# Attention inside two quantized feed-forward layers: Q and K in one step of row tiles, V and P·V moved between the quarters of a head pair

## The reference

```python
x = x + 0.5 * ffn(layernorm(x), w_gate, w_up, w_down)      # first layer
x = x + attn(layernorm(x), ...)                            # attention
x = x + 0.5 * ffn(layernorm(x), w_gate, w_up, w_down)      # last layer

# ffn: every operand is rounded to an 8-value grid in blocks of 16
h = silu(q(x) @ q(w_gate).T) * (q(x) @ q(w_up).T)          # 352 wide
return q(h) @ q(w_down).T

# attn: 16 heads of 64
q, k, v = x @ w_q, x @ w_k, x @ w_v                        # 128 -> 1024 each
attn = softmax(q @ k.T / 8)
y = (attn @ v) @ w_proj + b_proj + x
return layernorm(y) * ln_gamma + ln_beta
```

## Time and profile before

| | |
|---|---|
| median of 3 runs | 2265.52 us (2261.74 to 2266.74) |
| the profiled execution | 2263.16 us, of which the span is 2261.4 us |
| TensorE busy | 2142.7 us, 95% of the span |
| VectorE busy | 1605.5 us, 71% |
| GpSimd busy | 1407.7 us, 62% |
| ScalarE busy | 1151.4 us, 51% |
| mean granted TensorE clock | 0.978 |

### The profile page before, as it was taken

The page is one execution under the profiler, slowest core; times in us unless marked ns, Lnnn a source line. Parts: engine busy times, 40 slices in busy tenths (PEclk is TensorE's granted clock), DMA queues, the critical chain, the costliest instruction groups (busy, mean ns, idle before and its releaser), DMA issues.

```text
span 2261.4 us, 38387 instructions
## 1 busy us (share of the span) xinstructions
PE 2142.7 (95%) x14537; PEld 1094.4 (48%) x14537; DVE 1605.5 (71%) x2609; ACT 1151.4 (51%) x1749; POOL 1407.7 (62%) x1289
## 2 busy tenths in 40 slices
PE   3899999999999999999999999999999999999974
PEld 2344444545445454545545454554544545454432
DVE  5565767767687786868777686877778687776634
ACT  2455554645555454555545455455555545454532
POOL 3365666757576675757756576675757667665642
PEclk8799999999999999999999999999999999999986
DMA  1000000000000000000000000000000000000000
GB/s 60 1 7 2 6 2 2 12 2 7 7 7 7 2 11 2 7 7 7 7 2 11 2 7 7 2 12 2 10 3 6 7 2 12 2 2 7 2 7 10
DMA packets 167493, 15.83 MB, mean 7 GB/s; under 512 B 148304, under 2 KB 166928, under 8 KB 167312
## 3 DMA queue, kind: packets, MB, share of 16 engines
q1 hardware_dynamic: 167312, 13.39, 5.1%
HBM read 7.03 MB, written 4.19 MB: 5 GB/s over the span
## 4 chain that ended last, share of the span: by engine, by line
PE 85%; DVE 6%; SPq 2%; issue 2%; POOL 2%; DMA 1%; ACT 1%; POOLq 0%; DVEq 0%
PE pS L934 23%; PE pO L961 20%; PE pM L918 9%; PE pX L946 5%; PE pM L1077 5%; PE pX L985 5%; PE pM L973 3%; PE LpF L333 2%; PE FpF L333 2%; SPq L568 2%; PE FpF L296 2%; PE LpF L296 2%; PE LpF L309 2%; PE FpF L309 2%; PE LpF L324 1%
## 5 line engine op out<-in xcount | busy, mean ns | idle before, releaser
L676 POOL TENSOR_TENSOR ES<-ES,E 128x512 f32<-128x512 f32 x512 | 654.9, 1300 | 217.1 <-ACT E L747 209.9
L747 ACT ACTIVATE E<-pS 128x1024 f32<-128x1024 f32 x512 | 523.2, 1022 | 459.9 <-PE pS L934 421.3
L799 DVE TENSOR_REDUCE nmax<-pX 128x2 fp32r<-128x1024 f32 x512 | 622.0, 1215 | 113.4 <-PE pX L946 98.4
L961 PE MATMUL pO<-E,VA 128*64 128x512 f32 x2048 | 552.3, 618 | 0.0
L670 POOL TENSOR_TENSOR ES<-E 128x512 f32<-128x512 f32 x256 | 321.9, 1279 | 247.5 <-ACT E L747 247.5
L918 PE MATMUL pM<-xf,w_raw 128*64 128x512 f32 x1024 | 267.1, 600 | 2.8 <-DVE QL L889 2.1
L934 PE MATMUL pS<-QH,KH 64*128 64x512 f32 x1024 | 255.9, 496 | 0.0
L946 PE MATMUL pX<-KH,QH 64*128 64x512 f32 x1024 | 241.0, 412 | 4.7 <-DVE nmax L799 3.3
L934 PEld LDWEIGHTS pS<-QH,KH 64*128 64x128 f32 x1024 | 95.5, 183 | 288.1 <-issue 269.3
L946 PEld LDWEIGHTS pX<-KH,QH 64*128 64x128 f32 x1024 | 186.3, 306 | 36.7 <-DVE nmax L799 8.0
L934 PE MATMUL pS<-SH,onesr 64*128 64x512 f32 x1024 | 203.6, 393 | 0.0
(11 more groups left out here) (178 smaller groups left out, 3000.0 us busy)
## 6 DMA issues: line engine op xcount, KB each, us to landing
RROW<-RC SPq DMA_DIRECT2D x512, 2.0 KB, 2.0
xin<-in_L_attn_x SPq DMA_DIRECT2D x16, 256.0 KB, 3.0
SH<-nmax SPq DMA_DIRECT2D x256, 2.0 KB, 2.0
LC<-LROW SPq DMA_DIRECT2D x256, 2.0 KB, 2.1
out<-X SPq DMA_DIRECT2D x16, 256.0 KB, 2.5
w_raw<-in_L_attn_w_q SPq DMA_DIRECT2D x1, 512.0 KB, 3.6
w_raw<-in_L_attn_w_k SPq DMA_DIRECT2D x1, 512.0 KB, 4.7
w_raw<-in_L_attn_w_v SPq DMA_DIRECT2D x1, 512.0 KB, 5.6
```

What stands on the lines that cost most here:

```text
L676: ins = g.tensor_tensor(ES[i % 3][:, hd, :], ES[i % 3][:, hd, :], E[s][:, hd, :], ALU.add)
L747: a.activation(E[s][:, :, :], pS[:, :, :], ACT.Exp).then_inc(s_exp, 1)
L799: v.tensor_reduce(nmax[px % 2][:, :, t:t + 1], pX[:, :, :], AX.X, ALU.max, negate=True).then_inc(s_max, 1)
L961: ins = pe_.matmul(pO[half(hd), :], VA[of][:, kt, j * 128 + 64 * hd:j * 128 + 64 * hd + 64], E[kt][:, hd, :], start=kt == 0, stop=kt == KT ...
```

## The change

1. **Q and K.** The two `per_head` steps go. In their place `query_key` makes queries and keys of a pair together, in the second quarter, in the format `F32R` and from split operands: the weights as `W[0]` (rounded) and `W[1]` (rest), the input as `xs[0]` and `xs[1]`, three products each. The 128 rows of the contraction are cut in two halves, each a row tile of 64 rows; one half writes `pM` (queries) while the other writes `pO` (keys), and in a second turn, after `for_maxima`, they swap. That is 12 matmuls of 64 rows by 128 columns by 512. ScalarE then copies `QH` and `KH` one behind the other, and VectorE makes `QL` and `KL` one behind the other.
2. **P·V.** Since `pO` now holds the keys of pair `i + 2` in the second quarter, P·V of blocks 0 and 1 both stand in the third, and the first of them waits for `s_klo`, that is, until `KL` has been made.
3. **V.** The rounds of V stand in the first quarter, behind the pieces, for seven of the eight rounds of a batch, and one in the fourth quarter of pair 0. Pair 5 has none (`v_place`).
4. **Projection.** `project` stands ahead of the feed-forward pieces of its quarter.
5. Buffers: three instead of four of `QH`, `QL`, `KH`, `KL`, `OT`; one `xf`; `F.xm` and `L.xm` are merged into `xn`. Once, at the start, ScalarE and VectorE split the weights; once per batch ScalarE copies the transposed input twice instead of once, and VectorE subtracts once.

```diff
+    def v_place(r):
+        c, k = r // 8, r % 8
+        p, s = ((-2, 0), (-1, 0), (0, 0), (0, 3), (1, 0), (2, 0), (3, 0), (4, 0))[k]
+        return PAIRS * c + p, 3 if c == 0 and k < 2 else s
...
                     for c in batch_at(FirstLayer, FirstLayer.xf, b, t):
                         act.wait_ge(s_xmT_ps, c + 1)
-                        a.activation(xf[c % 2][:, :], F.pF[:, :], ACT.Copy).then_inc(s_xf, 1)
+                        a.activation(xs[0][:, :], F.pF[:, :], ACT.Copy)
+                        a.activation(xf[:, :], F.pF[:, :], ACT.Copy).then_inc(s_xf, 1)
...
-                        if s == 0 and there(i + 2, NP):
-                            act.wait_ge(s_q, i + 3)
-                            a.activation(QH[(p + 2) % 4][:, :], pM[:, :], ACT.Copy, scale=SCALE).then_inc(s_qhi, 1)
                         if s == 1 and there(i + 2, NP):
-                            act.wait_ge(s_k, i + 3)
-                            a.activation(KH[(p + 2) % 4][:, :], pM[:, :], ACT.Copy).then_inc(s_khi, 1)
+                            act.wait_ge(s_qk, i + 3)
+                            a.activation(QH[(i + 2) % 3][:, :], pM[:, :], ACT.Copy, scale=SCALE).then_inc(s_qhi, 1)
+                            a.activation(KH[(i + 2) % 3][:, :], pO[:, :], ACT.Copy).then_inc(s_khi, 1)
...
-                def per_head(k, p, x):
-                    for hd in range(2):
-                        ins = pe_.matmul(pM[half(hd), :], w_raw[:, k, p * 128 + 64 * hd:p * 128 + 64 * hd + 64], x,
-                                         start=True, stop=True)
-                    return ins
+                def query_key(i, p, turn):
+                    cols = slice(p * 128, p * 128 + 128)
+                    if turn == 1:
+                        pe.wait_ge(s_side, i + 1)
+                    for n, (w, x) in enumerate(((0, 0), (0, 1), (1, 0))):
+                        for side in range(2):
+                            k = (side + turn) % 2
+                            ins = pe_.matmul((pM, pO)[k][:, :], W[w][half(side), k, cols], xs[x][half(side), :],
+                                             start=turn == 0 and n == 0, stop=turn == 1 and n == 2)
+                    ins.then_inc(s_side if turn == 0 else s_qk, 1)
...
                         if kt == 0:
                             wait(pe, s_ot, i)
+                            pe.wait_ge(s_klo, min(i + 3, NP))
...
                         if s == 0:
                             times_v(i - 1, (p - 1) % PAIRS, KT - 1)
-                        else:
-                            times_v(i, p, s - 1)
-                        if s == 0 and there(i + 2, NP):
...
-                            per_head(0, p2, x).then_inc(s_q, 1)
-                        if s == 1 and there(i + 2, NP):
-                            pe.wait_ge(s_qlo, i + 3)
-                            per_head(1, p2, x).then_inc(s_k, 1)
+                        if s == 2:
+                            times_v(i, p, 0)
+                            times_v(i, p, 1)
+                        if s == 3:
+                            times_v(i, p, 2)
+                        if s == 1 and p % 2 == 1 and there(i - 4, NP):
+                            project(i, p)
                         first_ffn(b, 4 * p + s)
                         last_ffn(b, 4 * p + s)
-                        if s == 1 and p % 2 == 1 and there(i - 4, NP):
-                            project(i, p)
```

More of the change, by code:

```diff
@@ L428, in steps, with rounds_until @@
                 body(b, p, b % 2)
+    def v_place(r):
+        c, k = r // 8, r % 8
+        p, s = ((-2, 0), (-1, 0), (0, 0), (0, 3), (1, 0), (2, 0), (3, 0), (4, 0))[k]
+        return PAIRS * c + p, 3 if c == 0 and k < 2 else s
     def rounds_at(i, s):
[L432 to L441 removed]
+        return [r for r in range(max(i - 8, 0), min(i + 9, ROUNDS)) if v_place(r) == (i, s)]
+    def rounds_until(i, s):
+        return sum(v_place(r) <= (i, s) for r in range(ROUNDS))
     with ExitStack() as scope:
@@ L470, in make_program @@
         ES = [m.sb(f"ES{i}", [128, 2, S]) for i in range(3)]
-        OT = [m.sb(f"OT{i}", [128, S]) for i in range(4)]
+        OT = [m.sb(f"OT{i}", [128, S]) for i in range(3)]
         ON = [m.sb(f"ON{i}", [128, S]) for i in range(2)]
@@ L539, in make_program @@
         s_yacc = m.sem("s_yacc")
+        raw = [E[k][:, :, :].rearrange("p h n -> p (h n)") for k in range(2)]
         with nc.Block() as block:
@@ L822, in first_ffn @@
                 def first_ffn(b, t):
+                    for c in batch_at(FirstLayer, FirstLayer.xf, b, t):
+                        dve.wait_ge(s_xf, c + 1)
+                        v.tensor_tensor(xs[1][:, :], F.pF[:, :], xs[0][:, :].bitcast(F32), ALU.subtract).then_inc(s_xlo, 1)
+                    for c in batch_at(FirstLayer, FirstLayer.down, b, t):
+                        if c == 0:
+                            for k in range(2):
+                                dve.wait_ge(s_whi, k + 1)
+                                v.tensor_tensor(W[1][:, k, :], raw[k], W[0][:, k, :].bitcast(F32), ALU.subtract).then_inc(s_wlo, 1)
                     for c, k in parts_at(FirstLayer, FirstLayer.max_h, b, t):
```

118 lines of the change are left out of this document (60 added, 58 removed).

## The result

The changed kernel takes **2294.76 us** (2292.96 to 2300.18, 4 runs), the kernel before took 2264.95 us beside it (2261.74 to 2266.74, 4 runs). The ratio is 1.0142, with a 95% interval of 1.0119 to 1.0165: slower by 30 us, where 45 were forecast. The profiled execution took 2293.12 us, of which the span is 2291.3; its mean granted clock is 0.982 (0.978 before).

The account below looks back on a forecast made before the run. TensorE's own stream was taken as the bound. Per batch -2.9 + 2.3 + 1.8 + 1.8 - 0.2 = +2.8 us, over 16 batches +45, plus 2 at the start, on 2263: 2310 us, range 2258 to 2350.

Parts of the forecast that it names:

- stream of Q and K: Per batch, 16 steps of 0.86 us replaced by 8 times 6 couples, two column-tile changes gone: -2.9 us.
- third quarter: Pairs 2 and 6: maxima wait for KH, P·V for KL, 1.0 us each; pair 4 about 0.3: +2.3 us.
- projection: Second quarter of odd pairs: project waits for the reduction of pX until 3.5 us; +1.8 us per batch.
- fourth quarter: Without V, too little cover: waits 0.5 in pair 6, 0.8 in pair 1, 0.1 in five others; +1.8 us.
- VectorE freed: VectorE no longer waits for QH in the first quarter; small waits behind it shrink: -0.2 us per batch.
- The couples: Two matmuls of Q and K in two row tiles, side by side like the scores: 0.235 us per couple.
- The chain inside the quarter: Pairs 2 and 6, last Q and K matmul through copies and differences: KH at 4.15 us, KL at 5.0.
- so pair 3's old wait is replaced: Pair 3's projection: its old 0.63 us wait for a late reduction, blamed on VectorE waiting for QH, gives way.
- Rival (A): All waits covered or shared, so the kernel gets faster: 2217 us with full cover; chance 0.15.
- Rival (B): VectorE becomes the bound in shortened fourth quarters: 2393 us if all seven lose 1.0, half of it 2350; chance 0.12.
- the start: Ahead of the first scores, one more copy, one subtraction and KH behind QH, uncovered: +2 us once.

Follow-up runs that it names:

- the best order: Changed kernel with V in the fourth quarter, projection behind the pieces and row sums ahead of the two P·V: 2216.84 us, ratio 0.9777.
- the keys first: Changed kernel with KH copied ahead of QH and KL made ahead of QL: 2281.29 us, ratio 1.0066.

## Why the prediction was right, and where it was off

Forecast 2310 in 2258 to 2350, slower with 0.79; measured 2294.76. The mechanism held: a shorter stream, and more waiting than that. Part of the agreement in size is luck, since two of the terms are sums of parts that were off in both directions, and an old wait that went away had no term.

| per batch, us | forecast | measured |
|---|---|---|
| stream of Q and K | -2.9 | -2.9 (8 x 0.37, second quarters in the best order) |
| third quarter | +2.3 | 2.06 in the third quarters of pairs 2, 4 and 6 |
| projection | +1.8 | 1.47 by moving it back |
| fourth quarter | +1.8 | 1.81 by moving V back, net of 0.4 lost in pair 3 |
| VectorE freed | -0.2 | not seen by itself |
| pair 3's old wait, fourth quarter | no term | -0.4 |
| sum | +2.8 | +2.39 |

The measured rows don't add up to the last one: two of them are what an edit gave back, and those edits change other quarters too.

- **The couples.** Forecast 0.235, measured 0.23, and in the second turn's first couple 0.33 (909.65 to 909.98). The quarter length came out (2.76 and 2.77) because I had let the second turn start late.
- **The chain inside the quarter**, from the last matmul of Q and K to `KL`, was right to 0.1 us (`KL` done at 4.90, forecast 5.0); the maxima started at 4.11 instead of 4.3. It is made of the durations of the old rows alone, since nothing in it depends on how the rest of the kernel runs.
- **Projection.** Right at pair 1 (3.49 for 3.5), wrong at pair 3, where I let the old wait of the earlier trace rows be replaced because VectorE no longer stands for `QH` in the first quarter. That wait did shrink over the kernel, from 105.4 to 21.6 us, but only some 0.3 us of it per batch had stood in this place in the old kernel's pair 3: a sum over the kernel was read as the cause of one wait. What took its place is a rounding that takes 1.70 instead of 0.88 in every batch, and in 3 of the 13 a wait for the transferred row sums. Pair 3's second quarter is 6.07 where it was 5.82. The step that failed is "so pair 3's old wait is replaced": it took VectorE's operations from the old rows, and one of them is 0.82 longer in the new order.
- **Fourth quarter.** Pairs 6 and 1 were much as the earlier trace rows said. Pair 6 gave up 0.44 of V's time in place of 0.5, and pair 1's wait, 0.8 in the forecast, appears a quarter later, ahead of the next maxima: pair 2's first quarter went from 4.50 to 5.21. Pair 5, for which I had 0.1, lost 0.52 in the same way (pair 6's first quarter, 3.24 to 3.76), and pair 2 some 0.3 in its fourth. The sum is right by luck: these are more than 1.8, and the experiment gives 1.81 because pair 3 lost 0.4 by the same move.
- **Rival (A)**, all covered, would have needed another order: 2217 was its time, and the kernel with the three edits takes 2216.84. That the two agree to 1 us is luck, since some 4 us of it is the start, and the batch is shorter by 2.7 with some waits left and an old one gone. That it was excluded here because the chains lie inside the quarter was right for the order as it stands. I hadn't seen that a piece of the same quarter, the row sums, could cover them.
- **Rival (B)** asked for the whole V to be lost in all seven fourth quarters. All seven became shorter, by 0.4 (pair 6) to 1.2 us (pair 3).
- **From the batch to the whole.** This is the larger part of the 15 us by which I was high. 2.8 was taken 16 times. But the loop's first two batches did not grow (248.2 us together before, 246.3 after), nor the last (114.2 and 114.4 until its end), and the start, for which I had added 2, came 1.2 earlier (79.8 and 78.6). So 13 x 2.39 = 31.1, -1.9, -1.2, +0.2, and +1.8 behind the loop, which I can't explain, make 30.0; the spans differ by 29.9. As the first scores vary by up to 5 us between kernels that do the same ahead of the loop, that term was below what could be forecast.

Open: whether GpSimd is what makes VectorE's rounding take 1.70 us in pair 3, as the traces suggest (below), and what made the first two batches shorter in the kernel before with its projection ahead. Not tried: a remedy for pair 3, which would be worth up to 1.2 us per batch by its wait in the best kernel.

## What to carry to other kernels

When a step is made faster by packing it into the array, look for what stands between its last matmul and the first reader of what is copied out. Here the gain was lost because nothing was left there, and it came back with an independent piece of the same length (the row sums) in that place. Waits priced from old rows along one chain (copy, difference, reduction) were right to 0.1 us, while "this engine will be on time now" was wrong, because a wait summed over the kernel was taken for the wait at one place, and an operation behind it took twice as long in the new order. The three waits at different places added to within 0.3 us per batch, so each could be tested alone. Before the gains of two edits are added, compare them quarter by quarter: two edits can remove the same wait, as V and the row sums did, and the sum can still look right. And a gain per round of a loop should be multiplied only by the rounds that are in the steady state.

## What was unexpected of the hardware

- One and the same rounding of 128x704 on VectorE takes 0.89 us or up to 1.70 in pair 3 (the rows at 923.57 and 925.31). While the long one begins, GpSimd runs a pass with two operands, which ends at 924.52:

```profile
923.13 1.39 POOL L209 TENSOR_TENSOR Lh<-Lh,Lqh_inv 128x704 f32<-128x704 f32 x1
```

  In the kernel before the same pass ended at 915.11, and the rounding, which began at 915.10, took 0.88. A tiny operation of 128x4, which elsewhere takes 0.17 us, took as long as GpSimd's addition of exponentials had still to run in the rows looked at here. This is also what makes pair 3's fourth quarter 5.38 instead of 4.26 in the kernel before (batch 4; `ON`, and V behind it, wait for the row in the middle):

```profile
658.42 2.49 POOL L676 TENSOR_TENSOR ES<-ES,E 128x512 f32<-128x512 f32 x2 [0.40 <-ACT E L747]
658.44 1.27 DVE L162 TENSOR_SCALAR ny_var<-ny_mv 128x4 f32<-128x4 f32 x1
...
660.45 1.08 PE L1077 MATMUL pM<-w_raw,xf 128*64 128x512 f32 x4 [1.23 <-DVE ON L880]
```

  In the next batch both start at 792.43, and the tiny operation takes 0.17. Pair 5's with the keys first is of the same kind: it begins 0.16 behind the start of an addition (948.46) and takes 1.15, and in the kernel after it begins 0.48 behind one (954.02) and takes 0.83. Pair 3's took 1.27 in the 5 long batches and 0.16 or 0.17 in the 8 others. In the trace of after 43 of the 128 roundings begin while GpSimd is idle, and all take 0.8 or 0.9; the 27 that begin 1.0 or 1.1 us ahead of the end of a pass or an addition take 1.7 to 1.9. It isn't so for every instruction of GpSimd: 14 roundings that begin 0.8 ahead of the end of a 128x4 one (L168) take 0.9. All this is seen together in the traces, and no run isolates it.
- Behind a wait the next step came 0.1 to 0.2 us later than without one: the second turn's first couple takes 0.33 instead of 0.23 to the next, and with the keys first the maxima that waited take 0.55 to P·V (906.46 to 907.01) instead of 0.32. No run isolates this either.
- The two copies `QH` and `KH` start 0.49 us apart (910.65, 911.14) though each lasts 0.60, so the second copy cost less here than its duration.
